# Two fused pair layers on one Trainium2 core: the third norm's roots in pairs of chunks, and work moved between VectorE, ScalarE, GpSimd and TensorE

## What is computed

```python
# layer 0
x  = layernorm(pair) * ln1_w + ln1_b
left, right = sigmoid(x @ left1) * (x @ left2), sigmoid(x @ right1) * (x @ right2)
p  = einsum('nsre,nkre->nske', left, right)
p  = layernorm(p) * ln2_w + ln2_b
x1 = pair + einsum('nrse,ez->nsrz', p, out_w) * sigmoid(einsum('nsrz,zy->nsry', x, gate))
# layer 1
left  = x1 @ W_left + b_left + x1 @ W_eq + b_eq
rsum  = sum over r of (x1 @ W_right + b_right)
o     = left * rsum * sigmoid(x1 @ W_gate + b_gate)
out   = layernorm(o @ W_out + b_out + x1) * ln_scale + ln_bias      # the third norm
```

## Time and profile before

| | us |
|---|---|
| median of 3 runs (lowest 101.87, highest 102.32) | 101.92 |
| the profiled execution's own time | 101.74 |
| its span, first to last instruction | 99.8 |

### The profile page before, as it was taken

How to read it: one execution, slowest core, us unless ns; L and a number is a source line. 1 busy time by engine, 2 the same in 40 slices (tenths; PEclk the granted TensorE clock), 3 DMA queues, 4 the chain that set the end, 5 groups by cost and what they waited for, 6 DMA issues and landing times.

```text
span 99.8 us, 3188 instructions
## 1 busy us (share of the span) xinstructions
PE 78.5 (79%) x1260; PEld 60.0 (60%) x1260; DVE 69.3 (69%) x276; ACT 64.5 (65%) x112; POOL 53.4 (54%) x69
## 2 busy tenths in 40 slices
PE   0977999689999999999799788999999579580000
PEld 0964877567878799844337466767776467470000
DVE  0567696936475820098899978599969986999500
ACT  0543977998876347779694969958967886631000
POOL 5148994799940050004458505964129589979300
PEclk9999999999999999999999999999999999999855
DMA  2999998000000000000000000000000526267996
GB/s 42 196 160 145 146 146 90 14 10 16 0 0 0 3 7 0 0 0 0 0 0 7 7 0 7 0 7 0 7 0 0 83 35 105 40 101 118 145 145 95
DMA packets 34078, 4.68 MB, mean 47 GB/s; under 512 B 33936, under 2 KB 34064, under 8 KB 34064
## 3 DMA queue, kind: packets, MB, share of 16 engines
q1 hardware_dynamic: 32304, 4.10, 33.4%
q10 hardware_dynamic: 1760, 0.38, 2.1%
HBM read 2.38 MB, written 2.10 MB: 45 GB/s over the span
## 4 chain that ended last, share of the span: by engine, by line
PE 33%; ACT 23%; DVE 21%; issue 10%; POOL 3%; ACTq 3%; DVEq 0%; POOLq 0%
PE bank L835 9%; PE bank L908 7%; PE bank L898 7%; DVE stats L608 5%; ACT L431 4%; ACT L580 3%; ACT std L431 3%; PE bank L820 2%; ACT sig L531 2%; POOL xc L309 2%; DVE st L733 2%; ACTq L423 2%; DVE stats L687 2%; DVE lr L623 2%; PE bank L948 2%
## 5 line engine op out<-in xcount | busy, mean ns | idle before, releaser
L370 POOL TENSOR_TENSOR t_tok<-p_sb,rstd 128x512 f32<-128x512 f32 x7 | 10.1, 1451 | 12.5 <-DVE rstd L693 9.5
L835 PE MATMUL bank<-lr_blk,xnT 64*128 64x256 f32 x128 | 15.7, 388 | 0.9 <-ACT xnT L442 0.9
L623 DVE TENSOR_TENSOR lr<-bank,sig_lr 128x512 f32<-128x512 f32 x16 | 10.9, 682 | 6.5 <-ACT sig_lr L451 6.5
L379 POOL TENSOR_TENSOR oT<-o_a,rsum 128x512 f32<-128x512 f32 x8 | 8.8, 1096 | 11.0 <-DVE o_a L727 11.0
L835 PEld LDWEIGHTS bank<-lr_blk,xnT 64*128 64x128 f32 x128 | 11.9, 186 | 3.3 <-ACT xnT L442 1.1
L687 DVE BATCH_NORM_STATS2 stats<-p_sb 128x6 f32<-128x64 f32 x64 | 8.6, 213 | 6.9 <-ACT p_sb L495 6.9
L451 ACT ACTIVATE sig_lr<-bank 128x512 f32<-128x512 f32 x16 | 9.5, 596 | 3.3 <-PE bank L835 3.1
L608 DVE BATCH_NORM_STATS2 stats<-x_tok 128x6 f32<-128x64 f32 x64 | 8.9, 214 | 1.7 <-DMA x_tok<-in_x 1.7
L399 POOL TENSOR_TENSOR sq<-lr,row_rep 128x512 f32<-128x512 f32 x7 | 9.2, 1323 | 0.9 <-DVE lr L751 0.6
L718 DVE SCALAR_TENSOR_TENSOR x1T<-bank,w_rep,u 128x128 f32<-128x128 f32 x32 | 9.2, 343 | 0.1
L309 POOL TENSOR_TENSOR xc<-x_tok,stats 128x512 f32<-128x512 f32 (+1 forms) x8 | 8.1, 1011 | 2.1 <-DVE stats L608 2.0
(11 more groups left out here) (100 smaller groups left out, 169.4 us busy)
## 6 DMA issues: line engine op xcount, KB each, us to landing
x_tok<-in_x SPq DMA_DIRECT2D x14, 128.0 KB, 4.3
out<-sq SPq DMA_DIRECT2D x7, 256.0 KB, 3.8
x_tok<-in_x SPq DMA_DIRECT2D x3, 64.0 KB, 3.0
w_rep<-in_weights ACTq DMA_DIRECT2D x4, 45.1 KB, 3.0
out<-sq ACTq DMA_DIRECT2D x1, 128.0 KB, 3.4
out<-sq SPq DMA_DIRECT2D x1, 128.0 KB, 4.8
x_tok<-in_x ACTq DMA_DIRECT2D x1, 64.0 KB, 2.8
scale_rep<-in_rows SPq DMA_DIRECT2D x1, 64.0 KB, 9.1
```

The lines of the kernel that those rows point to most:

```text
L370: nc.gpsimd.tensor_tensor(t_tok[:, c % 2], by_token(p_sb[:, :, s]), by_token(rstd[:, 1:2, s]).to_broadcast([P, SPC, CH]), ALU.mult).then_i ...
L379: nc.gpsimd.tensor_tensor(oT[:, c % 2].rearrange("p (b k) -> p b k", b=BLK), o_a[:, c % 2].rearrange("p (b k) -> p b k", b=BLK), rsum[:, c ...
L623: nc.vector.tensor_tensor(lr[:, :, s].rearrange("p f (b q) -> p b f q", q=GRP), src[:, :, 2 * CH:4 * CH], sig_lr[:, j % 3].rearrange("p (b ...
L835: last = nc.tensor.matmul(dst, xnT[half, c, k * P:(k + 1) * P], lr_blk[half], start=True, stop=True, skip_group_check=True)
```

## The change

- The third norm's roots are grouped (0, 1), (2, 3), (4, 5), (6), (7) in place of (0), (1, 2, 3), (4, 5), (6), (7). The visits of the roots stay 5, 7 and 9, and those of the reciprocals 6 and 8. At visits 5 and 7 ScalarE now squares y ahead of the root and its table load.
- VectorE takes over two copies of the transposed t (chunks 4 and 6, at visits 4 and 6) and four right sums (chunks 1, 2, 4 and 6, at visits 3, 4, 6 and 8) from ScalarE.
- GpSimd scales chunks 0 to 3 in place of 0 to 2, and its scale-and-bias pairs stand at other places: chunk 0 ahead of `times_right` of visit 6, chunk 1 behind it, chunk 2 ahead of that of visit 8, chunk 3 behind it.
- Chunk 5 joins chunks 6 and 7: TensorE forms its scaled y a second time (at visit 8, in PSUM banks Q; chunk 6 moves to TT and XT, and chunk 7's sums follow to TT), and VectorE normalises it out of PSUM. Its `weigh3` and `scale3` go. `times_right(7)` on GpSimd waits for that y as well.

The core of the diff:

```diff
-ROOTS3 = [(0, 1), (1, 4), (4, 6), (6, 7), (7, 8)]
+ROOTS3 = [(0, 2), (2, 4), (4, 6), (6, 7), (7, 8)]
 ROOT3_AT = {5: [0], 7: [1], 9: [2]}
 INVERSE3_AT = {6: [0], 8: [1]}
-BIAS_FIRST = {8: [1]}
-BIAS_AT = {6: [0], 8: [2]}
-ON_VECTOR = (3, 4, 5, 6, 7)
-ON_POOL = (0, 1, 2)
+BIAS_FIRST = {6: [0], 8: [2]}
+BIAS_AT = {6: [1], 8: [3]}
+ON_VECTOR = (4, 5, 6, 7)
+ON_POOL = (0, 1, 2, 3)
+SUMS_ON_VECTOR = (1, 2, 4, 6)
+T_ON_VECTOR = (4, 6)
...
+                if c == CHUNKS - 1:
+                    pool.wait_ge(ys_ps, 1)
...
-                if i < CHUNKS:
+                if i < CHUNKS and i not in T_ON_VECTOR:
                     evacuate_tT(i)
...
+                if i in (5, 7):
+                    evacuate_y(i - 3)
...
-                if 0 <= i - 1 < CHUNKS:
+                if 0 <= i - 1 < CHUNKS and i - 1 not in SUMS_ON_VECTOR:
                     sums_of_right(i - 1)
...
+            def sums_of_right(c):
+                dve.wait_ge(rs_ps, c + 1)
+                b = sums_bank(c)
+                nc.vector.tensor_scalar(two(rsum[:, c]), bank[:, b:b + 2, HALF:HALF + 2], right_bias[:], None, ALU.add
+                                        ).then_inc(rs_ready, 1)
+
+            def evacuate_tT(c):
+                dve.wait_ge(tT_ps, c + 1)
+                dve.wait_ge(q_ps, c - 1)
+                nc.vector.tensor_copy(tT[:, c % 2], bank[:, TT]).then_inc(tT_ready, 1)
...
-            scale3(3)
             variance3(6)
             inverse3(2)
             scale3(4)
-            scale3(5)
+            dve.wait_ge(rstd3, 3)
+            normalise3(5, 0)
+            normalise3(5, 1).then_inc(scaled, 1)
...
+                if i == CHUNKS:
+                    pe.wait_ge(out_scaled, 2)
+                    pe.wait_ge(x1_ready, BLK * (CHUNKS - 1) + 1)
+                    centre_scaled_y(CHUNKS - 3)
...
+                if i in (CHUNKS, CHUNKS + 1):
+                    project_scaled_y(i - 3)
                 if i - 1 < CHUNKS:
                     project_sums(i - 1)
-                if i == CHUNKS + 1:
-                    project_scaled_y(CHUNKS - 2)
+                if i == CHUNKS:
+                    project_scaled_crossed(CHUNKS - 3)
```

More of the change, by code:

```diff
@@ L244, in sums_bank @@
         def sums_bank(c):
-            return GL if c < CHUNKS - 1 else Q
+            return GL if c < CHUNKS - 1 else TT
         def scaled_banks(c):
-            return Q if c == CHUNKS - 2 else GL
+            return {CHUNKS - 3: Q, CHUNKS - 2: TT, CHUNKS - 1: GL}[c]
         def quarter(b, t, k, h, n):
@@ L414, in _ @@
                     bias3(c)
-            for c in (3, 4, 5, 6):
+            for c in (4, 5, 6):
                 bias3(c)
@@ L573, in _ @@
                     root3_of(b)
-                if 0 <= i - 3 < CHUNKS and i != CHUNKS + 1:
+                if 0 <= i - 3 < CHUNKS and i not in (5, 7, CHUNKS + 1):
                     evacuate_y(i - 3)
-                if 0 <= i - 1 < CHUNKS:
+                if 0 <= i - 1 < CHUNKS and i - 1 not in SUMS_ON_VECTOR:
                     sums_of_right(i - 1)
@@ L755, in normalise3 @@
             def normalise3(c, h):
-                dve.wait_ge(ys_ps, c - CHUNKS + 3)
+                dve.wait_ge(ys_ps, c - CHUNKS + 4)
                 lo = c * SPC + h * SPC // 2
@@ L769, in _ @@
                     residual0(i - 1)
+                if i - 2 in SUMS_ON_VECTOR:
+                    sums_of_right(i - 2)
                 if i == 1:
                     inverse2(1)
+                if i in T_ON_VECTOR:
+                    evacuate_tT(i)
                 if i == 4:
@@ L775, in _ @@
                     inverse3(b)
-                if 0 <= i - 4 < CHUNKS:
+                if 0 <= i - 4 < CHUNKS - 3:
                     weigh3(i - 4)
@@ L1017, in centre_y @@
                     pe.wait_ge(g_ready, GATE0_ORDER.index(7) + 1)
-                elif c < CHUNKS - 1:
+                elif c < CHUNKS - 2:
                     pe.wait_ge(y_ready, c)
@@ L1043, in project_scaled_crossed @@
             def project_scaled_crossed(c):
-                pe.wait_ge(ys_straight, c - CHUNKS + 3)
+                pe.wait_ge(ys_straight, c - CHUNKS + 4)
                 project_tiles(c, scaled_banks(c), wout_scaled, 1).then_inc(ys_ps, 1)
@@ L1064, in _ @@
                     project_q(i)
+                if i == CHUNKS:
+                    pe.wait_ge(out_scaled, 2)
+                    pe.wait_ge(x1_ready, BLK * (CHUNKS - 1) + 1)
+                    centre_scaled_y(CHUNKS - 3)
                 if i == CHUNKS + 1:
-                    pe.wait_ge(out_scaled, 2)
                     pe.wait_ge(rs_ready, CHUNKS)
```

## The result

The changed kernel takes 100.9 us (median of 4 runs, 100.71 to 101.11) against 101.9 us for the kernel before beside it (101.81 to 102.32). The ratio is 0.989, with a 95% interval of 0.985 to 0.992: faster by 1.1%, about 1.0 us. The forecast was 100.95. The profiled execution took 100.71 us, with a span of 98.8.

The account below looks back on a forecast made before the run. The end was taken to follow chunk 4's transfer start, then saturated transfers. Loop +0.45 and tail -1.4 gave -0.95 us; the profiled 101.74 becomes 100.8, the median 100.95, range 100.4 to 101.6.

Parts of the forecast that it names:

- What bounds the kernel: The end follows the start of chunk 4's transfer, after its GpSimd bias at 90.72, then 7.35 us of saturated transfers.
- The tail: From the last sigmoid's start to the end of chunk 4's bias, 7.21 us before; claimed to shorten by 1.4 us.
- The hold-up: VectorE products of two SBUF operands and GpSimd products delay each other; avoiding it saves 1.0 to 1.1 in scale3(4).
- The loop: The pipeline of visits up to the last sigmoid; claimed 0.45 us later, 83.95 instead of 83.51.
- the walk: Visit-by-visit timing of the changed kernel from profile rows; gated products at 59.46, 64.0, 67.72, 72.84, 76.57 and 81.72.
- Visits 6 and 8 lose: ScalarE's square waits for y ahead of the table load; gain falls to 0.44 at visit 6, used up at 8.
- Visit 9's charge of 0.26: TensorE's 0.94 us for chunk 5's scaled y starts project_1(7) at 82.79 rather than 82.53.
- The prices that no row had: VectorE's cost for a copy of t, 0.56 us (bounds 0.5 to 0.69), and a right sum, 0.11 to the next start.
- The sum: 0.45 - 1.4 = -0.95 us for chunk 4's bias, ending at about 89.77; saturated 7.35 us stay; time 100.95.
- VectorE did not become the bound: Rival: VectorE's added copies and sums land on the path at full price; about 102.5 us, chance 0.07.
- TensorE's y is not on the path in full: Rival: TensorE's new 0.94 us comes onto the path in full rather than 0.26; 101.6 us, chance 0.09.
- the hold-up went: Rival: scale3(4) still meets times_right(7) on GpSimd or is long for another cause; 101.95 us, chance 0.06.

Follow-up runs that it names:

- the two doubled biases: Changed kernel with chunk 4's bias added twice on GpSimd, 101.91 us; with chunk 7's added twice on VectorE, 100.62 us; kernel before 101.97.
- the help alone: Kernel before, with only VectorE's two copies of t and four right sums put in: 101.05 us against 101.78, ratio 0.994.
- the load first: Changed kernel with ScalarE's square of chunks 2 and 4 again behind the root of visits 6 and 8: 99.89 us against 101.84 before, ratio 0.982.
- the tail's other order: Table load ahead of the square, plus chunks 4 and 5's root and products ahead of chunk 6's square and sum of squares: 99.23 us against 101.78 before.
- The padded kernels: Changed kernel with 32 or 80 tiny matmuls added beside the early warm-up matmuls: 103.53 and 106.63 us against 101.97 before.

## Why the prediction was right

- **What bounds the kernel** (chunk 4's issue and then saturated transfers): shown by the two doubled biases.
- **The tail, -1.4**: `scale3(4)` 0.69 (0.7 to 0.77 foreseen), chunk 4's bias 1.27 (1.27). The hold-up as cause is shown by the two products that are long again, and end some 0.55 us after GpSimd's instruction, with chunk 3's scaling back, and by the bias beside `scale3(5)`. The kernel with chunk 3's scaling back loses the whole gain, but in the traces only 0.43 us of the loss is the hold-up.
- **The loop, +0.45**: measured +0.33 on the last sigmoid, with the products of visits 3 to 8 within 0.12 us of the walk. Visits 6 and 8 lose for the reason given. Visit 9's charge of 0.26 for TensorE's extra y was 0.18 in the changed kernel, by the kernel without it; between the help alone and the load first it is 0.28.
- **The prices that no row had**: the copy of t takes 0.68 to 0.69 on VectorE, with the next instruction 0.61 to 0.67 behind its start, and a right sum 0.22, with 0.14 to the next start (69.88 to 70.02). I had 0.56 and 0.11 to the next start. The estimates from "VectorE: DVE Perf Modes" of the Trainium skill (section on the trn2 errata, at one column per cycle), 0.66 and 0.13, were the nearer. It hardly mattered, since the copies lie beside table loads.
- **The sum**: chunk 4's bias ended at 89.61 where 89.77 was foreseen. Two steps behind chunk 4's bias failed. The prediction let y of chunk 7 feed the last transfer only, but on VectorE its sum of squares stands ahead of chunk 6's product, and chunk 6 came 2.07 us after chunk 5 instead of 1.27. And the saturated transfers were not unbroken: a dip, whose cause is open, cost some 0.13. That the forecast fits to 0.05 us is in part luck: chunk 4's bias 0.16 earlier than foreseen and the dip cancelled.
- **The rivals**: VectorE did not become the bound (the help alone makes the kernel 0.6% faster), TensorE's y is not on the path in full, and the hold-up went.

## What to carry to other kernels

When the end is a saturated queue, find the transfer that opens the saturated stretch and shorten the chain to that one alone; work on later ones may even be put behind it, as the tail's other order did. A change that gathers several moves can hide one that costs: here taking one step back out (the order of square and table load) was worth 0.8 us in the traces, nearly as much as the whole change. Before an engine is asked to wait for data ahead of a table load, look whether the load can run during that wait.

## What the runs showed of the hardware

TensorE stops at fixed counts of its instructions. In every kernel here with a gap of this kind it stands at a multiple of 256 from the others (behind 2180, 2436, 2692 and 2948 instructions), whatever the matmul. Whether it stops depends on how fast it ran through the 256 before. In the twelve traces all stops of 0.18 to 1.17 us stand behind blocks that took 2.2 to 3.3 us from the first start to the last (2.71 and 2.65 in the changed kernel); two more such blocks, of 2.73 and 3.00 us, are followed by 0.04 and 0.06. No block of 3.5 us or more is followed by a stop, as the 3.74 and 3.55 us ahead of the same two counts in the kernel before. The profile's instruction queue moves blocks of 16 KB, ten of them for 2648 instructions and eleven for 2968. In the changed kernel two of them start at 82.08 and 85.67, some 1 us after TensorE has passed the counts 1924 and 2180 (81.19 and 84.54), and it goes on behind the two gaps 2.5 and 2.6 us after they started. The Trainium skill, "Advanced Engine Details and Errata", section "ISA Cache", gives a cache line as 16 KB, or 256 instructions. The trace agrees with the count, and adds the wait. The padded kernels show that it is the count; that TensorE waits for the next block is read from these times. So 64 small matmuls more or less can move a stop of up to 1.2 us onto the path or off it, with no change in the work.

And TensorE's clock: behind 1.78 us of idle time the granted clock was 0.50 for some 3 us in the traced run of one kernel, and three of its six runs have the lower mean clock of 0.95. Idle times of 1.19 us in visit 6 of the same run, and of 0.94 in the same visit of the changed kernel, left it at 1.00.
